# A tiled convolution whose column pairs and transposes take turns in two PSUM banks, with a tile's row arithmetic in two parts on VectorE

## The reference

```python
f = fftshift(fft2(x))                      # per channel
amp, phase = abs(f), angle(f)
gate = sigmoid(amp @ w_h + b_h) + sigmoid(amp @ w_l + b_l)
spatial = real(ifft2(ifftshift(amp * gate * exp(1j * phase))))
conv = conv2d(spatial, w_f, 3x3, 'SAME') + b_f
y = silu(conv) + x
z = (y - mean(y)) * rsqrt(var(y) + 1e-3) * gamma + beta   # over the channels
out = mamba_block(z)                       # the second block
```

## Time and profile before

| | us |
|---|---|
| median of 3 runs (4245.84 to 4251.49) | 4249.27 |
| the profiled execution: its time | 4248.45 |
| the profiled execution: its span | 4246.5 |

### The profile page before, as it was taken

How to read it: one execution, slowest core, us unless ns; L and a number is a source line. 1 busy time by engine, 2 the same in 40 slices (tenths; PEclk the granted TensorE clock), 3 DMA queues, 4 the chain that set the end, 5 groups by cost and what they waited for, 6 DMA issues and landing times.

```text
span 4246.5 us, 94479 instructions
## 1 busy us (share of the span) xinstructions
PE 3975.6 (94%) x31687; PEld 2858.3 (67%) x31687; DVE 3487.8 (82%) x8772; ACT 3152.6 (74%) x4936; POOL 2582.5 (61%) x2713
## 2 busy tenths in 40 slices
PE   7998899899989994899999999999999999999998
PEld 4787578758875883566666666666666666666665
DVE  4568557754876384899999999999999999999997
ACT  4445534553555253899999999999999999999997
POOL 0036104600560065688888888888888888888886
PEclk9999999999999997999999999999999999999999
DMA  2013101400240022111111111111111111111110
GB/s 91 1 53 129 58 9 61 161 11 12 73 157 0 14 85 77 36 40 40 42 40 42 40 37 42 40 42 40 40 39 40 42 40 42 40 37 42 40 42 26
DMA packets 214857, 205.85 MB, mean 48 GB/s; under 512 B 14368, under 2 KB 149152, under 8 KB 214688
## 3 DMA queue, kind: packets, MB, share of 16 engines
q1 hardware_dynamic: 214688, 203.60, 14.8%
HBM read 136.45 MB, written 67.11 MB: 48 GB/s over the span
## 4 chain that ended last, share of the span: by engine, by line
PE 59%; ACT 0%; DVE 0%; POOL 0%; issue 0%; POOLq 0%; DVEq 0%; ACTq 0%
PE g_ps L1084 7%; PE g_ps L1069 6%; PE g_ps L1027 6%; PE g_ps L1013 5%; PE g_ps L1072 5%; PE g_ps L1101 5%; PE g_ps L1044 3%; PE g_ps L1114 3%; PE g_ps L1120 3%; PE g_ps L1093 3%; PE g_ps L1053 3%; PE g_ps L1018 3%; PE g_ps L1033 2%; PE g_ps L1109 2%; PE g_ps L1006 2%; PE g_ps L1038 1%
## 5 line engine op out<-in xcount | busy, mean ns | idle before, releaser
L1396 DVE TENSOR_TENSOR g_mmat<-g_emat,g_ps 128x1024 f32<-128x1024 f32 x512 | 598.9, 1210 | 1.3 <-PE g_ps L1044 1.3
L1235 ACT ACTIVATE g_emat<-g_ps 128x1024 f32<-128x1024 f32 x512 | 521.3, 1025 | 86.3 <-PE g_ps L1072 84.8
L1339 DVE SCALAR_TENSOR_TENSOR g_acc<-g_ps,g_conv_w,g_acc 128x504 f32<-128x504 f32 (+1 forms) x768 | 554.5, 722 | 10.9 <-ACT g_acc L1198 9.2
L914 POOL TENSOR_TENSOR g_acc<-g_acc,g_tap 128x508 f32<-128x508 f32 x384 | 482.2, 1270 | 126.1 <-DVE g_acc L1339 126.1
L654 POOL MEMSET f_s_hi<- 128x192 f32 x4 | 1.0, 258 | 761.0 <-PE f_ps L345 761.0
L1084 PEld LDWEIGHTS g_ps<-g_mmat,g_dtx 128*32 128x32 f32 x8192 | 192.8, 109 | 310.4 <-issue 213.4
L1069 PE MATMUL g_ps<-g_rz,g_l 128*128 128x512 f32 x1024 | 391.3, 463 | 1.6 <-DVE g_z L1424 1.6
L229 PE MATMUL f_ps<-f_s_hi,f_wf_hi 128*128 128x256 f32 x1152 | 360.6, 313 | 4.9 <-DVE f_s_lo L489 4.9
L1084 PE MATMUL g_ps<-g_mmat,g_dtx 128*32 128x128 f32 x8192 | 329.3, 279 | 0.0
L230 PE MATMUL f_ps<-f_s_lo,f_wf_hi 128*128 128x256 f32 x1152 | 326.6, 284 | 0.0
L424 ACT ACTIVATE f_s_hi<-f_ps 128x384 fp32r<-128x384 f32 x256 | 125.6, 491 | 270.5 <-PE f_ps L217 265.2
(11 more groups left out here) (193 smaller groups left out, 12319.1 us busy)
## 6 DMA issues: line engine op xcount, KB each, us to landing
f_xt<-in_x_cols SPq DMA_DIRECT2D x32, 1024.0 KB, 10.9
f_xres<-in_x SPq DMA_DIRECT2D x128, 256.0 KB, 2.8
z<-f_zout SPq DMA_DIRECT2D x128, 256.0 KB, 2.0
g_zin<-z SPq DMA_DIRECT2D x128, 256.0 KB, 2.6
g_zres<-z SPq DMA_DIRECT2D x128, 256.0 KB, 2.9
out<-g_outb SPq DMA_DIRECT2D x128, 256.0 KB, 2.9
f_wf_raw<-in_w_f SPq DMA_DIRECT2D x1, 576.0 KB, 7.1
g_wx<-in_in_proj_t SPq DMA_DIRECT2D x1, 192.0 KB, 2.4
```

What stands on the lines that cost most here:

```text
L914: pool.tensor_tensor(acc[:, j, :, 1:], acc[:, j, :, 1:], tap1[:, j, :, 0:P - 1], ALU.add).then_inc(add_p[j], 1)
L1235: act.activation(emat[:, g, :].rearrange("p (b n) -> p b n", b=2), ps[:, D_BANK[g]:D_BANK[g] + 2, :], ACT.Exp).then_inc(e_a[g], 1)
L1339: dve.scalar_tensor_tensor(out=acc[:, j, :, k:], in0=four(ps[:, bank, :])[:, :, 0:P - k], scalar=conv_w[:, j, 3 - k:4 - k], in1=acc[:, j, ...
L1396: dve.tensor_tensor(mmat[:, g, :].rearrange("p (h n) -> p h n", h=HEADS), emat[:, g, :].rearrange("p (h n) -> p h n", h=HEADS), ps[:, CB, ...
```

## The change

Units run seven ahead of a tile rather than five, and bank 7 is used by units too. Of a tile's four units the first, third and fourth go to bank 6 and the second to bank 7, between the two halves of the transposes. DVE's rows of a tile are cut in two (`tile_rows` up to row 1, and `tile_ends`), with the second half of the residual, a low part and the second half of the moments between them. ACT's `middle` moves ahead of the second half of `center`. The last three transposes of an image have banks of their own.

```diff
+AHEAD = 7
+def unit_bank(u):
+    return (6, 7, 3, 4, 5, 6, 7)[u] if u < AHEAD else (6, 7, 6, 6)[(u - AHEAD) % 4]
+def turn_bank(k, h):
+    return 7 if k < BATCHES - 2 else (7, 6, 0, 1)[2 * (k - BATCHES + 2) + h]
 # PE, columns(b, u)
-                if u == 5:
-                    pe.wait_ge(lo_ready, b * UNITS + 1)
-                if u > 5:
-                    pe.wait_ge(lo_ready, b * UNITS + u)
+                n, k = (u - AHEAD) % 4, (u - AHEAD) // 4
+                if 5 <= u < AHEAD:
+                    pe.wait_ge(lo_ready, b * UNITS + (u - 4))
+                elif u >= AHEAD and n == 1:
+                    if k >= 2:
+                        pe.wait_ge(ysum_done, b * PARTS + (2 * (k - 2) + 2))
+                    else:
+                        pe.wait_ge(lo_ready, b * UNITS + (u - 3 if k else u - 1))
+                elif u >= AHEAD:
+                    pe.wait_ge(lo_ready, b * UNITS + (u - 1 if n == 2 else u))
 # PE, turn(b, k, h)
-                pe.wait_ge(ysum_done, b * PARTS + (2 * k + h + 1))
+                if h == 1 and used < UNITS:
+                    pe.wait_ge(lo_ready, b * UNITS + (used + 1))
+                if k < BATCHES - 2 or (k, h) == (BATCHES - 2, 0):
+                    pe.wait_ge(ysum_done, b * PARTS + (2 * k + h + 1))
 # PE, conv(b, k)
-                    if n == 3 and k >= 2:
-                        turn(b, k - 2, 1)
                     mm = position(k, p)
...
-                    if n < 4 and 4 * k + 5 + n < UNITS:
-                        columns(b, 4 * k + 5 + n)
+                    if n == 3 and k >= 2:
+                        turn(b, k - 2, 1)
+                    unit = 4 * k + AHEAD + min(n, 3) if n not in (3, 5) else UNITS
+                    if unit < UNITS:
+                        columns(b, unit)
 # ACT
                     for n in range(4):
-                        if 4 * k + 5 + n < UNITS:
-                            hi_part(4 * k + 5 + n)
+                        if 4 * k + AHEAD + n < UNITS:
+                            hi_part(4 * k + AHEAD + n)
                         if n == 0 and 1 <= k <= BATCHES:
                             silu(k - 1)
+                        if n == 2 and k < BATCHES:
+                            middle(k)
                         if n in (1, 2) and k >= 3:
                             center(k - 3, n - 1)
...
-                    if k < BATCHES:
-                        middle(k)
 # DVE, tile_rows up to row 1, then tile_ends
+                if k >= 2:
+                    dve.wait_ge(vT_mm, b * PARTS + (2 * k - 2))
...
+            def tile_ends(b, k):
...
                 for k in range(BATCHES + 1):
-                    for n in range(4):
-                        if 4 * k + 5 + n < UNITS:
-                            lo_part(b, 4 * k + 5 + n)
-                        if n in (0, 2) and k >= 2:
-                            residual(b, k - 2, n // 2)
-                            moments(b, k - 2, n // 2)
+                    if k >= 2:
+                        residual(b, k - 2, 0)
+                    for n in range(3):
+                        if 4 * k + AHEAD + n < UNITS:
+                            lo_part(b, 4 * k + AHEAD + n)
+                        if n == 0 and k >= 2:
+                            moments(b, k - 2, 0)
                     if k < BATCHES:
                         tile_rows(b, k)
+                    if k >= 2:
+                        residual(b, k - 2, 1)
+                    if 4 * k + AHEAD + 3 < UNITS:
+                        lo_part(b, 4 * k + AHEAD + 3)
+                    if k >= 2:
+                        moments(b, k - 2, 1)
+                    if k < BATCHES:
+                        tile_ends(b, k)
```

More of the change, by code:

```diff
@@ L265, in _, with row_transform @@
                 pe.sem_inc(one)
-            def row_transform(b):
+            def row_transform(b, after):
                 for t in range(8):
@@ L269, in row_transform @@
                     for j in range(4):
+                        if t == 0 and j == 3 and after:
+                            pe.wait_ge(ysum_done, b * PARTS - 1)
                         pe.wait_ge(y_free[j], b * 8 + (t + 1))
@@ L348, in image @@
                     pe.wait_ge(t_free[j], b * 8 + 8)
-                for u in range(5):
+                for u in range(AHEAD):
                     columns(b, u)
@@ L356, in image @@
                 if not last:
-                    row_transform(b + 1)
-            row_transform(0)
+                    row_transform(b + 1, True)
+            row_transform(0, False)
             with pe.Fori(0, IMAGES - 1) as b:
@@ L418, in hi_part @@
                     act.wait_ge(s_mm, b * UNITS + (u + 1))
-                    at, bank = 2 * u % RING, (6, 7, 3, 4, 5)[u] if u < 5 else 6
+                    at, bank = 2 * u % RING, unit_bank(u)
                     if at == 0 and u:
@@ L494, in tile_rows @@
                 done = b * BATCHES + (k + 1)
-                first, ends = ps[:, 3 * (k % 2), :], ps[:, 3 * (k % 2) + 2, :]
+                first = ps[:, 3 * (k % 2), :]
                 y = conv_y[:, k % 2]
@@ L507, in tile_rows @@
                                          op0=ALU.mult, op1=ALU.add)
+            def tile_ends(b, k):
+                done = b * BATCHES + (k + 1)
+                ends = ps[:, 3 * (k % 2) + 2, :]
+                y = conv_y[:, k % 2]
+                near, far = slice(0, 256), slice(256, 512)
                 dve.wait_ge(conv_mm, done)
@@ L521, in residual @@
                     dve.wait_ge(ln_done, b * PARTS + (n - 3))
-                dve.tensor_tensor(ysum[:, n % 4, :], ps[:, 7, :], xres[:, n % 4, :], ALU.add).then_inc(ysum_done, 1)
+                dve.tensor_tensor(ysum[:, n % 4, :], ps[:, turn_bank(k, h), :], xres[:, n % 4, :], ALU.add).then_inc(ysum_done, 1)
             def moments(b, k, h):
```

7 lines of the change are left out of this document (5 added, 2 removed).

## The result

The changed kernel takes 4282.41 us (median of 4 runs, 4276.30 to 4287.43), the kernel before 4248.35 (4 runs on the same chip): ratio 1.0079, 95% interval 1.0062 to 1.0097. It is slower, by some 34 us. Its profiled execution takes 4284.11 us, 35.7 more than that of before. Forecast were 4273 us, and 24.6 more than the profiled execution of before.

The account below looks back on a forecast made before the run. DVE's own work (about 9.9 us) plus a round trip through the one bank for units bounded the loop. Per image -6.4 + 8.8 + 3.75 = +6.15, four images +24.6 on 4248.45: 4273 us, its own range 4262 to 4284.

Parts of the forecast that it names:

- The collision: Steady tiles: POOL's gamma multiply starts 0.2 us before DVE's row 1, adding 0.95 us per tile; chance throughout 0.72.
- The loop: Steady tiles: a round through bank 7's residual takes 11.54 us, 12.5 with row 1 stretched; ten tiles +8.8 per image.
- First tiles: Tiles 0 to 3: early units let PE set the pace, sums of tile 3 at 269.8; -6.4 us per image.
- End of an image: Tiles 13 to 15: without units the loop opens, POOL runs through both rows; 29.7 against 25.95, +3.75 us per image.
- the last transposes' own banks take PE out of the wait for it: Image's end: PE no longer waits for the last residual, but DVE's row-transform copies still do; claimed effect nothing.
- Row 1 first: Steady tiles: DVE's row 1 starts before POOL's gamma multiply; -2.4 us per image, 4239 us; chance 0.15.
- Only some tiles: Steady tiles: POOL and row 1 collide only in some, as starts drift; about half the cost, 4256 us; chance 0.09.
- The freed PE: Steady tiles: two banks free PE from the residual's chain; -1.6 us per tile, some 4160 us; chance 0.04.

Follow-up runs that it names:

- resid_first: Changed kernel with DVE's first-half residual ahead of the previous tile's tile_ends and both halves of center behind ACT's fourth high part; 4204.71 us, ratio 0.9890.
- pool_one_column: Changed kernel with POOL's gamma multiply and beta add done on one element per partition instead of 512; 4198.47 us, ratio 0.9879.
- last_turns_bank7: Changed kernel with the last three transposes of an image in bank 7 again, with the waits of the kernel before; 4273.67 us, ratio 1.0058.
- turn_after: resid_first with the first half of PE's transposes behind the first product instead of ahead of it; 4188.67 us, ratio 0.9861.
- act_center_last: Changed kernel with the second half of ACT's center behind the fourth high part instead of behind middle; 4246.86 us, ratio 0.9991.
- turn_after_b7: turn_after with the last transposes of an image back in bank 7; 4183.19 us, ratio 0.9846.
- ahead5: Changed kernel with units five ahead of a tile instead of seven, banks, waits and row order as changed; 4339.36 us, ratio 1.0216.

## Why the prediction was right, and where it was off

**The collision.** Right, and shown from both sides: with POOL later, or POOL short, row 1 is 0.65 and a tile loses its extra microsecond. The forecast put POOL 0.2 us ahead of row 1; it is 0.15 to 0.17 in most steady tiles and up to 0.28 in the others, and row 1 takes 1.63 to 1.65 in all of them. No run shifted POOL's start by a few tenths, so how near the edge lies is not shown. The Trainium skill (page "SBUF — State Buffer", section "Who interferes with whom") left open who follows when POOL queues behind row 2; the trace says POOL does, 1.65 instead of 0.64.

**The loop.** 12.42 measured, 12.5 forecast, and link by link as summed: 0.73, 3.76, 0.70, 3.16, 2.36 and 1.71 against 0.72, 3.74, 0.70, 3.16, 2.38 and 1.79. The residual of bank 7 closes it: PE's unit waits for it in every steady tile, 0.6 us in most where the text had said about a microsecond, and with `tile_ends` out of that round (resid_first) this wait is gone and a tile takes 10.55, against 11.4 to 11.8 with the collision alone removed. The other wait of PE, 1.38 ahead of the transposes, is not in the prediction; it is not on the loop, since PE waits again for the residual behind it. That the ten tiles cost +8.7 where +8.8 was forecast is in part luck: a tile is 0.07 shorter than forecast, and the ring-wrap rows, taken as free, cost 0.6 per image.

**First tiles.** -6.3 against -6.4; sums of tile 3 at 270.22 (269.8 forecast).

**End of an image.** +3.6 to +5.2 against +3.75; pool_one_column shows that POOL's long instructions set it, as the text had it, but part of their price is one that the text did not have: PE's wait of 3.2 to 3.6 us behind the stretched rows and the lower clock after it. Tile 15's sums come 12.8 to 13.1 us behind tile 14's where the clock is at 0.73 to 0.74 between them, 11.85 in image 1 where it is at 0.86, against 11.1 forecast. The last tile takes 7.0 and not 7.8, which by luck hides some of that.

**What was mis-sized.** The step "the last transposes' own banks take PE out of the wait for it, but DVE's copies of the row transform stand behind the same residual: nothing". The copies do stand there; but PE, let in early, stops again and restarts at the lower clock. Behind the last residual +11.1 was measured. last_turns_bank7 gives back 6.1 us of it (1.3 + 2.0 + 2.8), and the same edit on turn_after 5.5 in the time. Of the rest, 3.5 is the clock in the second block, and 1.5 the second fall, which comes in some images and not in others; no run ties either of them to the change. The forecast also let the next image shift with the last row in full; the last residual came 0.4 to 1.6 us nearer to it in three images.

**The rivals.** Row 1 first (4239) is what act_center_last makes true by an order: 4247. Only some tiles (4256) is out: row 1 is stretched in every steady tile. The freed PE (4160) is what turn_after and turn_after_b7 come near to, 4183 to 4189: the engines had the room, as that rival said, and it was the orders of DVE, ACT and PE that kept it shut.

## What to carry to other kernels

Follow a loop's round link by link, every wait and every instruction queued ahead of the waited-for one: that gave the tile to 0.1 us, and the next order's tile (resid_first) too. Before two engines' instructions are moved, write down who of them starts first where both work in SBUF; here POOL started 0.15 us ahead, and that meeting cost 36 to 41 us in the steady tiles of four images (act_center_last, pool_one_column). And letting an engine start early is worth nothing if it must stop again for the same thing: look at what clock it restarts with.

## What had not been expected of the hardware

A wait of 1.83 to 2.30 us on PE was followed by the lower clock in 31 of 40 tiles, one of 1.37 to 1.59 us at the same place in none of 40 (ahead5 against the changed kernel); the slow restart cost 1.3 us, more than the longer wait. And the same wait left the clock at 1.00 in nine tiles, among them the first steady tile of every image; the rows beside the other five do not tell why.
